# Router logits with the experts in the partitions, turned back by small products, and the key transposes behind the first gate product

## The chip, the cores and the metric

The kernel runs on one NeuronCore of one Trainium2 chip. A core has five engines that run their own instruction queues and wait for each other through semaphores: TensorE (PE in the profile, with its weight loads as PEld), VectorE (DVE), ScalarE (ACT), GpSimd (POOL) and SyncE (SP), which here only starts transfers. The metric is the time of one execution on the device, in microseconds; less is better. A "stationary" operand is the one that TensorE loads as weights, a "moving" operand is streamed past it.

## The reference

Sixteen sequences of 256 tokens with 256 channels go through an attention layer and then a mixture of experts, each with a residual sum. What matters for this change is the router, which for each token gives eight logits:

```python
logits_h = x @ wt.T                       # x: tokens x 256, wt: 8 x 256
logits_g = jnp.repeat(g @ wg.T, s, axis=0)
logits = (logits_h + logits_g / GE_TEMP) / (1.0 + 1.0 / GE_TEMP)
scores = jax.nn.softmax(logits, axis=-1)
topk_w, topk_idx = jax.lax.top_k(scores, K)      # K = 2, then normalised
```

The experts (eight, and two shared blocks) are all computed, as gate, up and down products with a leaky ReLU between, and weighted by the router's result. Everything is float32. For the products of the attention, of the router and of the gate and up matrices the kernel splits each operand into a leading part "hi" and a rest "lo" of a type that TensorE takes at full rate, and sums hi·hi + lo·hi + hi·lo.

## The kernel before

The 4096 tokens are worked in eight rounds of 512 tokens (four tiles of 128, `TILES`), two sequences a round. Attention of round r and the experts of round r - 1 are interleaved by hand: each engine has one function `attention(r, moe, following)`, which issues the attention's instructions of round r and, between them, those of the experts of round `moe` = r - 1. Round 0 is written out with no experts, rounds 1 to 6 are one hardware loop, round 7 is written out again, and the experts of round 7 follow alone (the tail). Nothing but this written order and the semaphores sets when an instruction runs.

At the head of each round, on TensorE: the normalised tokens `x1` of the round before are turned (`turn_x1`, L1405) into banks psG and psO; queries of tile 1 (`q_half`, L63 to L65 through the helper `products`) and half of tile 2; the router's `logits`; four transposes of the keys `kd` into psO (L1271), which first wait until VectorE has read the logits out of psG and psO; the first block's gate product (`gate(moe, 0)`) into psG; the second half of query tile 2; the first up product (`up(moe, 0)`); and so on up to the score loop, which takes most of a round (`score`, `turn`, `value`, with the rest of the experts between).

The logits before the change: for each of 4 tiles and 2 channel halves three products with the tokens stationary (128 x 128) and 256 columns of `Wall` moving, of which the first 8 are the router's; 24 products. They stand with tokens in the partitions, so that the softmax over experts runs along the free axis.

VectorE at the same place: keys normalised into `kd`, `MK`, then `router_logits` (L1077 twice adds `cond_logits`, L1081 takes the maximum, L1082 subtracts it: `lgc<-lg,lgx`, both inputs in SBUF), `sum_q` of query tile 1 (L1017), the key parts `KB` (L902, L906), `leak(0)` (L1132), `hidden(0)` (L1142), `sum_q` of tile 2, `router_best`, and further to the first `scores` (L1042), where the score loop begins for it.

ScalarE: `route` (x1T), squares and copies of query tile 0 and 1 (L619, L623), `softmax` (L696), key copy (L628), `take_gate(0)` (L707), query tile 2. GpSimd: powers `rk` and `rq` (L541), then `scale_q` of tile 0 (L385, 128 x 1024, both inputs in SBUF), and in the score loop the normalisation of the attention's rows. `scale_q` of tile 0 starts after the power of tile 0, which starts after VectorE's `sum_q` of tile 0.

SyncE's queue matters in the tail: `experts` loads gate and up weights when the up product that used their buffer is done, then writes the router's weights `WT` to memory and reads them back broadcast, row by row, as `Wb`.

## Time and profile before

| | us |
|---|---|
| median of 3 timed runs | 1135.3 |
| lowest, highest | 1133.45, 1136.15 |
| the profiled execution | 1139.32 |
| its span, first to last instruction | 1137.4 |
| PE busy in the span | 1028.3 (90%) |
| PEld, DVE | 843.4, 781.0 |
| ACT, POOL | 526.0, 443.3 |
| mean granted TensorE clock | 0.976 of full |

The profile is of one execution, which took 4.0 us more than the median of the timed ones. Busy shares are averages over stages; what bounds a stage is read from the timeline of that stage, where each row may carry the idle time in front of it and the engine that ended it.

### The profile page before, as it was taken

To read this page: it belongs to the slowest core of one execution; us is meant where nothing else is said; L and a number is where in the kernel's file an instruction comes from. 1 tells how busy PE (TensorE), PEld (TensorE's weight loads), DVE (VectorE), ACT (ScalarE), POOL (GpSimd) and SP (SyncE) were. 2 spreads that over 40 slices of the span, in tenths; PEclk is the share of its full clock that TensorE was granted. 3 is DMA by queue.
4 is the path that set the end of the run, shared out by engine and by line. 5 is a ranking of instruction groups with operands and counts; after the bars stand their busy time and mean duration, and the time that the engine had idled before them with its cause. 6 is when DMAs were issued, how large, how long until landed. Compare 5 with 4: busy or idle time off the path is not lost.

```text
span 1137.4 us, 22612 instructions
## 1 busy us (share of the span) xinstructions
PE 1028.3 (90%) x7340; PEld 843.4 (74%) x7340; DVE 781.0 (69%) x2538; ACT 526.0 (46%) x1563; POOL 443.3 (39%) x422
## 2 busy tenths in 40 slices
PE   2377899999999999899999999899998999999898
PEld 1265587777877788677877787777877778777777
DVE  6768858775687648775587747876597756866442
ACT  2048724663356614655255623565146642566111
POOL 3154414553435505453336424354145433355112
PEclk9688999999999999999999999999999999999999
DMA  5064411321123212321123111221113211232033
GB/s 203 19 177 158 150 38 56 104 85 57 40 80 98 66 40 74 103 66 38 58 91 96 59 55 58 92 68 65 59 56 103 84 38 33 81 103 65 20 104 119
DMA packets 40939, 89.89 MB, mean 79 GB/s; under 512 B 4128, under 2 KB 18976, under 8 KB 40304
## 3 DMA queue, kind: packets, MB, share of 16 engines
q1 hardware_dynamic: 40816, 88.29, 24.3%
q8 instruction: 73, 1.20, 0.5%
q14 instruction: 50, 0.41, 0.1%
HBM read 78.67 MB, written 11.70 MB: 79 GB/s over the span
## 4 chain that ended last, share of the span: by engine, by line
PE 66%; DVE 20%; issue 6%; ACT 5%; POOL 1%; DMA 1%; SPq 1%; DVEq 0%; ACTq 0%; POOLq 0%
PE psY L1460 11%; PE psO L1393 6%; PE psS L1363 5%; PE psG L63 4%; PE psG L65 4%; PE psG L64 4%; PE psT L1374 3%; PE psS L63 3%; PE psS L64 3%; DVE work L1042 3%; PE psS L65 3%; PE psS L1358 2%; PE psO L1396 2%; PE psT L63 2%; PE psT L65 2%
## 5 line engine op out<-in xcount | busy, mean ns | idle before, releaser
L552 POOL TENSOR_TENSOR work<-work,rden 128x514 f32<-128x514 f32 x128 | 134.3, 1049 | 329.1 <-DVE rden L1023 328.5
L1460 PE MATMUL psY<-Wd,H 128*128 128x256 f32 x640 | 166.7, 395 | 3.7 <-POOL H L566 3.7
L675 ACT ACTIVATE work<-work,low 128x257 f32<-128x257 f32 x256 | 128.3, 503 | 80.7 <-DVE low L1042 80.6
L63 PE MATMUL psG<-x1T_hi,Wgu 128*128 128x512 f32 x280 | 128.1, 458 | 11.7 <-ACT leaky L707 9.8
L1460 PEld LDWEIGHTS psY<-Wd,H 128*128 128x128 f32 x640 | 113.3, 189 | 32.3 <-issue 15.6
L1042 DVE CUSTOM_DVE_ANT_0 work<-psS,bias,null_s 128x256 f32<-128x256 f32 x256 | 113.0, 478 | 18.3 <-PE psS L1363 18.0
L1132 DVE SCALAR_TENSOR_TENSOR leaky<-leaky 128x512 f32<-128x512 f32 x80 | 55.6, 695 | 101.5 <-ACT leaky L707 100.5
L541 POOL TENSOR_TENSOR rq<-qss,neghalf 128x16 f32<-128x16 f32 x32 | 93.7, 2930 | 55.0 <-DVE qss L1017 55.0
L65 PE MATMUL psG<-x1T_lo,Wgu 128*128 128x512 f32 x280 | 110.3, 394 | 0.0
L64 PE MATMUL psG<-x1T_hi,Wgu 128*128 128x512 f32 x280 | 109.6, 391 | 0.0
L667 ACT ACTIVATE qT_hi<-psO 128x256 fp32r<-128x256 f32 x128 | 48.9, 382 | 108.8 <-PE psO L1396 107.7
L679 ACT ACTIVATE work<-work,low 128x129 f32<-128x129 f32 x256 | 99.2, 389 | 0.0
L566 POOL TENSOR_TENSOR H<-H,Wb 128x512 f32<-128x512 f32 x64 | 82.5, 1289 | 41.9 <-DMA Wb<-wscr 30.0
L1393 PE MATMUL psO<-PTs,kvs 128*64 128x256 f32 x512 | 84.0, 405 | 10.6 <-DVE qT_lo L1069 10.6
L687 ACT ACTIVATE PTs<-psT 128x512 f32<-128x512 f32 x128 | 75.3, 588 | 35.7 <-PE psT L1374 35.6
L558 POOL TENSOR_TENSOR rstd<-ve,neghalf 128x1 f32<-128x1 f32 x32 | 17.5, 546 | 186.9 <-DVE ve L987 186.9
L1363 PE MATMUL psS<-KB_hi,qT_hi 64*128 64x256 f32 (+1 forms) x512 | 84.5, 321 | 0.0
L1374 PE MATMUL psT<-ident,work 128*128 128x128 f32 x512 | 78.0, 275 | 5.3 <-ACT PTs L687 4.2
L554 POOL TENSOR_TENSOR work<-work,rden 128x258 f32<-128x258 f32 x128 | 79.4, 620 | 0.0
L1069 DVE TENSOR_TENSOR qT_lo<-psO,qT_hi 128x256 fp32r<-128x256 f32 x128 | 53.7, 420 | 37.2 <-ACT qT_hi L667 37.2
L1048 DVE CUSTOM_DVE_ANT_0 work<-psS,bias,null_s 128x128 f32<-128x128 f32 x256 | 78.9, 345 | 0.0
L1374 PEld LDWEIGHTS psT<-ident,work 128*128 128x128 f32 x512 | 62.2, 140 | 22.5 <-issue 7.9
(242 smaller groups left out, 2677.4 us busy)
## 6 DMA issues: line engine op xcount, KB each, us to landing
Wgu<-wexp SPq DMA_DIRECT2D x80, 512.0 KB, 3.5
Wb<-wscr SPq DMA_DIRECT2D x64, 256.0 KB, 3.7
wexp<-Wgu SPq DMA_DIRECT2D x10, 512.0 KB, 2.9
xin<-in_x SPq DMA_DIRECT2D x8, 512.0 KB, 4.1
xres<-in_x SPq DMA_DIRECT2D x8, 512.0 KB, 5.0
out<-work SPq DMA_DIRECT2D x8, 512.0 KB, 3.1
H<-in_wgu SPq DMA_DIRECT2D x10, 256.0 KB, 3.8
bscr<-bscr SPq DMA_DIRECT2D x1, 2048.0 KB, 13.0
```

The costliest lines, as they stand in the source:

```text
L63: te.matmul(dst, a_hi, b_hi, start=start, stop=False)
L64: te.matmul(dst, a_lo, b_hi, start=False, stop=False)
L65: return te.matmul(dst, a_hi, b_lo, start=False, stop=stop)
L541: pool.tensor_tensor(rq[:, t, :], qss[:, t, :], neghalf[:], ALU.pow).then_inc(rq_done.sem, 1)
L552: pool.tensor_tensor(T1[sl][:, hs, :], T1[sl][:, hs, :], rden[sl][:, 1, hs].unsqueeze(2) .to_broadcast([P, 2, N + 1]), ALU.mult)
L675: act.activation(T1[sl][:, h, :], T1[sl][:, h, :], ACT.Exp, scale=-1.0, bias=low[sl][:, 1, h:h + 1], accum_out=den[sl][:, 1, h:h + 1])
L679: last = act.activation(T0[sl][:, h, :], T0[sl][:, h, :], ACT.Exp, scale=-1.0, bias=low[sl][:, 0, h:h + 1], accum_out=den[sl][:, 0, h:h + 1])
L1042: ins = dve.tensor_tensor_reduce(T1[sl][:, h, 0:N], psS[:, i, 0:N], bias[:, h0 + h, :], 1.0, null_s[:, 2 * bb + 1, h0 + h:h0 + h + 1], ALU ...
L1363: mm = te.matmul(psS[:, i, first:first + keys_], qT[a][half, p, q1:q1 + P], KB[b][half, bb, 0:keys_], start=False, stop=(first == N and b ...
L1374: mm = te.transpose(psT[:, 0, (2 * i + j) * P:(2 * i + j + 1) * P], T1[sl][:, 2 * s + i, j * P:(j + 1) * P], ident[:])
L1393: te.matmul(psO[i * DH:(i + 1) * DH, 0:N], kvs[:, 2 * bb, DH:2 * DH], PT[n % 2][:, i, 0:N], start=True, stop=False)
L1460: mm = te.matmul(psY[:, t // 2, (t % 2) * D:(t % 2 + 1) * D], H[:, k % H_RING, t * P:(t + 1) * P], Wd[:, ORDER[k], :], start=(k == 0 and t ...
```

## The change

The router's weights get a tile of their own, `WtP`, with the 8 hi and the 8 lo columns side by side. They become stationary and the 512 tokens stream past: two products of 16 columns with `x1T` hi (one per channel half) and two of 8 columns with `x1T` lo, all into psO, 16 partitions x 512 tokens. ScalarE copies these to `LT` in SBUF. Four small float32 products with `LT` stationary and `I2` (two 8 x 8 identities on top of each other, so that it also adds the hi and the lo rows) moving give 128 tokens x 8 experts per tile, in psY. The first gate product stands between the logits and these small products; the key transposes come behind them. On ScalarE the new copy stands where the softmax stood, and the softmax moves behind `take_gate(0)`. In the tail VectorE issues `leak(0)` ahead of `router_best` and `hidden(0)` ahead of `router_weights`, and ScalarE's `softmax` and `weights` stand behind its first and second gate copy. One small VectorE instruction that makes `I2` is added to the preparation.

```diff
@@ -135,8 +135,10 @@
-        Wall = [sb(f"Wall_{part}", [P, KC, E + KVN + HEADS * DH], F32R) for part in PARTS]
-        KV0, Q0 = E, E + KVN
+        Wall = [sb(f"Wall_{part}", [P, KC, KVN + HEADS * DH], F32R) for part in PARTS]
+        KV0, Q0 = 0, KVN
+        WtP = sb("WtP", [P, KC, 2 * E], F32R)
+        I2 = sb("I2", [2 * E, E])[:]
...
+        LT = sb("LT", [2 * E, TOK])[:]
+        WT = LT[0:E, :]
...
@@ act: attention
                     if t >= 2 and moe is not None:
                         take_gate(moe, t - 2)
+                        if t == 2:
+                            softmax(moe)
...
                     if t == 1:
                         if moe is not None:
-                            softmax(moe)
+                            logits(moe)
...
+            def logits(m):
+                need(act, lt_ps, m, 1)
+                need(act, wscr_in, m - 1, 16)
+                act.activation(LT, psO[0:2 * E, :], ACT.Copy).then_inc(lt_done.sem, 1)
...
             route(ROUNDS - 1)
-            softmax(ROUNDS - 1)
-            weights(ROUNDS - 1)
+            logits(ROUNDS - 1)
             for k in range(BLOCKS):
                 take_gate(ROUNDS - 1, k, True)
+                if k == 0:
+                    softmax(ROUNDS - 1)
+                if k == 1:
+                    weights(ROUNDS - 1)
...
@@ dve: preparation, router_logits, tail
                 dve.wait_ge(pre_t.sem, 4)
+                pre(dve.tensor_tensor(I2, ident[0:2 * E, 0:E], ident[0:2 * E, E:2 * E], ALU.add))
...
-                for i, bank in enumerate((psG, psO)):
+                for i in range(BB):
                     ins = dve.tensor_tensor(
-                        lg[:, 2 * i:2 * i + 2, :], bank[:, :].rearrange("p (t c) -> p t c", t=2)[:, :, 0:E],
+                        lg[:, 2 * i:2 * i + 2, :], psY[:, 0, 2 * i * E:2 * (i + 1) * E].rearrange("p (t e) -> p t e", t=2),
...
             router_logits(m)
+            leak(m, 0)
             router_best(m)
+            hidden(m, 0, True)
             router_weights(m)
-            for k in range(BLOCKS):
+            for k in range(1, BLOCKS):
...
@@ te: attention
                 if moe is not None:
                     logits(moe)
+                    gate(moe, 0)
+                    turn_logits(moe)
                 need(te, kd_done, r, 1)
-                if moe is not None:
-
-                    te.wait_ge(vchain["router"].ev.sem, vchain["router"].ev.at(moe, 1))
...
                 mm.then_inc(kdT_ps.sem, 1)
-                if moe is not None:
-                    gate(moe, 0)
                 q_half(2, 1).then_inc(q_ps.sem, 1)
...
             def logits(m):
+
                 need(te, x1T_v, m, 3)
+                for c in range(KC):
+                    te.matmul(psO[0:2 * E, :], WtP[:, c, :], x1T[0][:, c, :], start=(c == 0), stop=False, skip_group_check=True)
+                for c in range(KC):
+                    mm = te.matmul(psO[0:E, :], WtP[:, c, 0:E], x1T[1][:, c, :], start=False, stop=(c == KC - 1),
+                                   skip_group_check=True)
+                mm.then_inc(lt_ps.sem, 1)
+
+            def turn_logits(m):
+
+                need(te, lt_done, m, 1)
+                need(te, ysum, m - 1, TILES)
                 for t in range(TILES):
-                    for c in range(KC):
-
-                        mm = products(te, (psG, psO)[t // 2][:, (t % 2) * 2 * P:(t % 2 + 1) * 2 * P],
-                                      [part[:, c, t * P:(t + 1) * P] for part in x1T],
-                                      [part[:, c, 0:2 * P] for part in Wall], c == 0, c == KC - 1)
+                    mm = te.matmul(psY[:, 0, t * E:(t + 1) * E], LT[:, t * P:(t + 1) * P], I2, start=(t == 0), stop=True,
+                                   skip_group_check=True)
                 mm.then_inc(lg_ps.sem, 1)
...
                 gate(m, k, True)
+                if k == 0:
+                    turn_logits(m)
                 up(m, k, True)
```

TensorE in the loop's round, before: the last tile's logits, then the key transposes, then the first gate product.

```order
L63 MATMUL psO<-Wall_hi,x1T_hi 128x256
L64 MATMUL psO<-Wall_hi,x1T_lo 128x256
L65 MATMUL psO<-Wall_lo,x1T_hi 128x256
L86 REGISTER_ALU
L1269 ISA
L1271 MATMUL psO<-ident,kd 128x128 x4
L86 ISA x2
L63 MATMUL psG<-x1T_hi,Wgu 128x512
```

The same place with the change (the first operand listed is not always the stationary one):

```order
L1427 MATMUL psO<-x1T_hi,WtP 16x512 x2
L1429 MATMUL psO<-x1T_lo,WtP 8x512 x2
L86 ISA x2
L63 MATMUL psG<-x1T_hi,Wgu 128x512
L64 MATMUL psG<-x1T_hi,Wgu 128x512
L65 MATMUL psG<-x1T_lo,Wgu 128x512
...
L1438 MATMUL psY<-I,LT 128x8 x4
L86 REGISTER_ALU
L1288 MATMUL psO<-ident,kd 128x128 x4
L63 MATMUL psT<-Wall_hi,xnT_hi 128x512
```

The gate product moved ahead of the key transposes, and what VectorE waits for (the end of L1438) now stands behind the gate product and behind a ScalarE copy.

ScalarE in the loop's round, before, from the copy of query tile 1 to the square of tile 2:

```order
L623 ACTIVATE work<-psS 128x1024
L696 ACTIVATE lex<-lgc 128x32
L86 REGISTER_ALU
L628 ACTIVATE KB_hi<-psO 64x512
L86 ISA
L707 ACTIVATE leaky<-psG 128x512
L86 REGISTER_ALU
L619 ACTIVATE work<-psT 128x1024
```

and with the change:

```order
L630 ACTIVATE work<-psS 128x1024
L86 ISA
L705 ACTIVATE LT<-psO 16x512
L86 REGISTER_ALU
L635 ACTIVATE KB_hi<-psO 64x512
L86 ISA
L719 ACTIVATE leaky<-psG 128x512
L709 ACTIVATE lex<-lgc 128x32
L86 REGISTER_ALU
L626 ACTIVATE work<-psT 128x1024
```

The copy to LT stands behind both large passes over query tile 1; the softmax moved behind the gate copy.

VectorE in the tail, before:

```order
L1082 TENSOR_TENSOR lgc<-lg,lgx 128x32
L1088 TENSOR_REDUCE lsum<-lex 128x4
...
L1099 MAX_INDEX topi<-top,score 128x8 x4
L1104 CAST topf<-topi 128x8
...
L1115 TENSOR_TENSOR oh<-wsel,trec 128x32
L1132 SCALAR_TENSOR_TENSOR leaky<-leaky 128x512
L1142 TENSOR_TENSOR H<-psS,leaky 128x512
```

and with the change:

```order
L1098 TENSOR_TENSOR lgc<-lg,lgx 128x32
L1148 SCALAR_TENSOR_TENSOR leaky<-leaky 128x512
L1104 TENSOR_REDUCE lsum<-lex 128x4
...
L1115 MAX_INDEX topi<-top,score 128x8 x4
L1158 TENSOR_TENSOR H<-psS,leaky 128x512
L1120 CAST topf<-topi 128x8
...
L1131 TENSOR_TENSOR oh<-wsel,trec 128x32
```

The first leaky ReLU and the first hidden product moved into the router's chain, ahead of the weights that TensorE's `turn_weights` waits for.

## Rows read from the trace of the kernel before

**Rows 1.** The page's chain that ended last: shares of the span by engine.
```profile
PE 66%; DVE 20%; issue 6%; ACT 5%; POOL 1%; DMA 1%; SPq 1%; DVEq 0%; ACTq 0%; POOLq 0%
```

**Rows 2.** Timeline, round 3: start us, us, engine, line, operation [idle before <-releaser]
```profile
430.78 0.28 PE L63 MATMUL psG<-Wall_hi,x1T_hi 128*128 128x256 f32 x1
...
433.96 0.17 DVE L1077 TENSOR_TENSOR lg<-psG,cond_logits 128x16 f32<-128x16 f32 x1 [0.68 <-PE psO L65]
...
434.35 0.66 PE L1271 MATMUL psO<-ident,kd 128*128 128x128 f32 x4 [0.54 <-DVE lg L1077]
434.55 0.19 DVE L1082 TENSOR_TENSOR lgc<-lg,lgx 128x32 f32<-128x32 f32 x1
...
434.87 1.91 POOL L385 TENSOR_TENSOR work<-work,rq 128x1024 f32<-128x1024 f32 x1
...
436.00 0.39 PE L65 MATMUL psG<-x1T_lo,Wgu 128*128 128x512 f32 x1
...
436.23 0.39 PE L63 MATMUL psT<-Wall_hi,xnT_hi 128*128 128x512 f32 x1
...
439.26 0.69 DVE L1142 TENSOR_TENSOR H<-psG,leaky 128x512 f32<-128x512 f32 x1 [0.50 <-PE psG L65]
```

**Rows 3.** Round 3, ScalarE's two passes over query tile 1, same columns.
```profile
431.78 1.03 ACT L619 ACTIVATE work<-psS 128x1024 f32<-128x1024 f32 x1 [2.99 <-DVE qss L1017]
...
432.71 1.02 ACT L623 ACTIVATE work<-psS 128x1024 f32<-128x1024 f32 x1
```

**Rows 4.** Groups by line: xcount | busy us, mean ns | idle before.
```profile
L701 ACT ACTIVATE WT<-psO 8x512 f32<-8x512 f32 x8 | 4.6, 573 | 4.9 <-PE psO L1421 4.9
```

**Rows 5.** Timeline of the preparation: float32 products with 16 moving columns.
```profile
48.44 1.89 PE L1186 MATMUL psT<-bias 128*128 128x16 f32 x8 [0.86 <-DVE bias L845]
```

**Rows 6.** Timeline, round 4: VectorE's logits beside GpSimd's scale_q, and hidden(0).
```profile
565.17 1.84 DVE L1082 TENSOR_TENSOR lgc<-lg,lgx 128x32 f32<-128x32 f32 x1
566.93 1.21 DVE L1017 TENSOR_REDUCE qss<-work 128x16 f32<-128x1024 f32 x1
...
571.06 0.69 DVE L1142 TENSOR_TENSOR H<-psG,leaky 128x512 f32<-128x512 f32 x1
...
565.05 1.91 POOL L385 TENSOR_TENSOR work<-work,rq 128x1024 f32<-128x1024 f32 x1
```

**Rows 7.** Timeline, round 2: the same two instructions.
```profile
304.37 0.19 DVE L1082 TENSOR_TENSOR lgc<-lg,lgx 128x32 f32<-128x32 f32 x1
...
304.52 1.91 POOL L385 TENSOR_TENSOR work<-work,rq 128x1024 f32<-128x1024 f32 x1
```

**Rows 8.** Timeline: VectorE's first scores in rounds 2, 3, 4; last x1 tile of round 3.
```profile
325.00 0.48 DVE L1042 CUSTOM_DVE_ANT_0 work<-psS,bias,null_s 128x256 f32<-128x256 f32 x1
...
455.18 0.48 DVE L1042 CUSTOM_DVE_ANT_0 work<-psS,bias,null_s 128x256 f32<-128x256 f32 x1
...
586.94 0.48 DVE L1042 CUSTOM_DVE_ANT_0 work<-psS,bias,null_s 128x256 f32<-128x256 f32 x1
...
554.80 0.49 DVE L994 SCALAR_TENSOR_TENSOR x<-x,rstd,xres 128x256 f32<-128x256 f32 x1 [0.34 <-POOL rstd L558]
```

**Rows 9.** Timeline, round 1: hidden(0).
```profile
178.51 0.69 DVE L1142 TENSOR_TENSOR H<-psG,leaky 128x512 f32<-128x512 f32 x1 [0.30 <-PE psG L65]
```

**Rows 10.** Timeline, the tail: logits, router chain, turn_weights, the third gate product.
```profile
1081.63 0.58 PE L63 MATMUL psG<-Wall_hi,x1T_hi 128*128 128x256 f32 x1 [1.98 <-DVE x1T_lo L1126]
...
1087.51 0.19 DVE L1088 TENSOR_REDUCE lsum<-lex 128x4 f32<-128x32 f32 x1 [0.30 <-ACT lex L696]
...
1090.93 0.19 DVE L1115 TENSOR_TENSOR oh<-wsel,trec 128x32 f32<-128x32 f32 x1
...
1091.55 0.53 PEld L1421 LDWEIGHTS psO<-ident,oh 128*8 128x8 f32 x4
...
1093.59 0.19 PEld L63 LDWEIGHTS psT<-x1T_hi,Wgu 128*128 128x128 f32 x1 [1.51 <-issue]
```

**Rows 11.** Stretch: us, each engine's busy us, granted TensorE clock, DMA share, GB/s.
```profile
1081.60:1085.40 3.80, 3.77 (x17) 3.77 (x18) 0.00 (x0) 0.00 (x0) 0.00 (x0) 0.50 0.00 0
```

## What the change will do to the time

> **What bounds the kernel now.** I read the chain of waits first: 66% of it is TensorE, 20% VectorE [rows 1]. That is a mean over stages, so the next view is the timeline of one loop round (round 3) from the logits on. TensorE issues the 24 logit products from 430.78; the last result frees VectorE at 433.96, after 0.68 us of idle time there, and the key transposes then wait 0.54 us for VectorE [rows 2]. So far TensorE leads. Then comes what decides. VectorE's next idle time is 0.50 us in front of `hidden(0)` at 439.26 [rows 2]. From there to its first `scores` at 455.18 [rows 8] it is idle only for hand-offs of 0.15 to 0.20 us in its own chains. So the stretch from 434 to 455 is VectorE's: TensorE could gain there 0.50 us of waiting that VectorE has, and no more.
>
> A second reading is in round 4. `lgc<-lg,lgx`, which takes 0.19 us in round 3, took 1.84 us, from 565.17 to 567.01. GpSimd's `scale_q` ran from 565.05 to 566.96 [rows 6]. In rounds 2 and 3 the same instruction began at 304.37 and 434.55, that is 0.15 and 0.32 us before `scale_q` at 304.52 and 434.87, and was not held [rows 2, 7]. Rounds 5 and 6 read like round 4, and in the written-out rounds 1 and 7 it came late in `scale_q` and was held briefly, to the same end. The sum over two inputs `lgc` therefore cannot run while `scale_q` does; the reduction behind it can (in round 3 it did), and so can the additions in front, which read one input from PSUM.
>
> The Trainium skill ("SBUF — State Buffer", section "Who interferes with whom") says why: a VectorE instruction with two SBUF inputs and a GpSimd instruction that reads SBUF want the same read port, and whichever starts first blocks the other for its whole length. By that rule, the trace agrees, with ends 0.05 us apart in round 4. It speaks against this change, since what counts is the order of the two starts. Nothing below needs this paragraph.
>
> What the hold costs: from the end of `scale_q` to the first scores are 586.94 - 566.96 = 19.98 us in the held round 4, with no idle time before `hidden(0)` [rows 6, 8]; rounds 5 and 6 give the same. In round 2 they are 325.00 - 306.43 = 18.57, in round 3 455.18 - 436.78 = 18.40 [rows 2, 7, 8]. So a hold costs 1.41 or 1.58 us. It is carried to the round's end: from the first scores to the last `x1` tile are 554.80 - 455.18 = 99.62 us in round 3 [rows 8], and 99.6 in each loop round, held or not.
>
> **The change, part by part.**
> - Logits, TensorE: 24 products of 256 columns at (433.96 - 0.42 - 430.78) / 23 = 0.12 us, 2.9 us in all [rows 2], where 0.42 is the last product's 0.28 and a hand-off of 0.14. They become 4 products of 512 columns at 436.23 - 436.00 = 0.23 us [rows 2], 0.9 us. TensorE saves 2.0 us a round, and the 0.54 us wait.
> - The added path: the logits are ready at about 430.78 + 0.9 + 0.3 = 432.0, but ScalarE is in its passes over query tile 1 until 432.71 + 1.02 = 433.73 [rows 3]. The copy to LT then takes 0.57 us, by the copy of 8 x 512 [rows 4], to 434.25. TensorE has finished the first gate product (431.7 + 6 x 0.23 = 433.1) and waits about 1.2 us. Queued behind that wait are the key transposes and `q_half`; VectorE waits in `router_logits`, with `sum_q` of tile 1 behind it.
> - The four small products: 4 float32 products with few columns are 8 instructions, which took 1.89 us at half clock in the preparation [rows 5], so some 1.0 us at full. The other bound is the transposes of keys, 4 in 0.66 us [rows 2]. No row has 8 columns from 16 partitions; I take 1.0, the nearest kind. The logits reach VectorE at 435.0 to 435.4, against 433.96: 1.0 to 1.4 us later.
> - What VectorE meets there: `lgc` starts 0.59 us behind (434.55 - 433.96 [rows 2]), at 435.6 to 436.0. GpSimd's `scale_q` runs from 434.87 to 436.78 and is not touched by the change. So `lgc` is held until 436.8, whichever bound is right. ScalarE's passes and `scale_q` both start from the same `sum_q` of tile 0, so this comes out the same in every loop round: **all five loop rounds with late starts (2 to 6) are held**, instead of three of five.
> - Sum for the rounds, on the profiled execution: rounds 2 and 3 lose 1.41 + 1.58 = 3.0 us; rounds 4 to 6 lose nothing, as VectorE leaves `lgc` at the same moment. In round 1 `scale_q` ends at about the moment at which the new `lgc` ends, and VectorE's 0.30 us of waiting before `hidden(0)` [rows 9] goes, since the up product is earlier; in round 7 it is 0.1. That gives back 0.4. TensorE's own 2.0 us a round are lost in waits for ScalarE and, at the second gate product, for VectorE's `hidden(0)`.
> - The moved softmax costs nothing: `router_best` reads it more than 4 us later. The new wait of the first down product on the router's first link is over 10 us old by then; likewise `ysum` before the small products.
> - Tail: the logits start at 1081.63 [rows 10], and the 24 products took to 1086.4. The granted clock was 0.50 of full (1.2 GHz) until 1085.4 [rows 11], after TensorE had waited. The four long ones take 4 x 0.43 = 1.8 us with the first start, to 1083.5. The gate product, four sixths at half clock, ends at 1085.85; the small products 1.0 later, VectorE's logits at 1086.95 against 1086.51. Its chain to the weights was 1091.12 - 1087.51 = 3.6 us [rows 10]; now `leak(0)` and `hidden(0)` lie inside it, 0.69 us each [rows 2], so the weights are done at about 1092.5. TensorE waits for them from 1090.8 and starts the third gate product at 1092.95, where it started at 1093.59 after a wait for ScalarE's gate copies [rows 10]. Gain 0.65; the transfer of the weights follows the third up product and moves by 0.9, so it does not take it back. I take 0.7, bounds 0.3 (if the small products are slower than thought) and 1.3 (the whole wait of 1.51 less a hand-off).
> - Preparation: one more small VectorE instruction in a chain in which each waits for the last. One with two small SBUF inputs takes 0.19 [rows 2]. I add 0.2.
>
> Sum on the profiled execution: 3.0 - 0.4 - 0.7 + 0.2 = +2.1 us, 1139.3 to 1141.4.
>
> **From there to the median.** The timed runs are 4.0 us shorter at the median and lie 2.7 us apart. The hold of the old kernel is decided by 0.1 to 0.3 us between two starts, so it will differ from run to run: five rounds, about 1.45 us each. With three held rounds in the median run the change costs 2.1, with two 3.5, with none 6.4, with all five it gives 0.8. Three missing holds would explain the 4.0 us alone, which speaks for few. I take two: 1135.3 + 3.5 = **1138.8**. A measurement can tell about 0.2%, 2.3 us: slower begins at 1137.6.
>
> **Rivals.**
> - The old kernel is held in three to five rounds when timed as well. Then +2.1 to -0.8, 1134.5 to 1137.4, within 0.2%. The profile (three of five) is for it, the shorter timed runs against.
> - TensorE is the bound after all. Place: the second half of query tile 2, at 436.23 before. It would start when the small products and key transposes are done, at about 435.5, so 0.7 earlier; seven rounds give 4.9, with tail and preparation 5.4: 1129.9. It decides only if VectorE is not later than before at `hidden(0)`. Against it: VectorE's time from `lgc` on has 0.5 us of air at most.
> - The idle gaps. TensorE now stops for 1.2 us in front of the small products and again at the second gate product. In the tail it came back at half clock after a wait of 1.98 us, the second of its kind in a row, and stayed there for 3.8 us; after the wait of 1.51 us it ran at full [rows 10, 11]. If the gaps bring that to seven rounds, 3.8 us at half speed is 1.9 us of work each, of which VectorE's lead hides some: up to 8 more, 1147.
> - The change does not do what it says about the hold (`lgc` slips in before `scale_q`): it would have to start before 434.87, hence need ScalarE 0.8 us sooner than its own rows allow. Then rounds 2 and 3 lose nothing, and 4 to 6 win 1.4 each: 1130.5.
>
> **Chances.** Forecast with at most two held rounds before: 0.53. Held three to five: 0.28. TensorE the bound: 0.09. Gaps: 0.06. No hold: 0.04. Faster by over 0.2%: 0.13; within 0.2%: 0.29; slower: 0.58. The range takes in none to all five held rounds and half of an error in the tail: 1133.9 to 1142.0.
>
> **What would show it.** Right: `lgc` of rounds 2 to 6 takes 1 us or more and ends within 0.1 us of `scale_q`; 19.98 us from there to the first scores; a loop round of 131.7 us throughout; VectorE's wait before `hidden(0)` gone; TensorE idle about 1.2 us before the small products. Wrong: `lgc` at 0.19 us; small products well over 1.0 us, when VectorE would leave after `scale_q`'s end and each tenth costs seven; a clock below full in the head of the rounds; or a tail that did not shorten.

## The result, and the profile after

| | median us | lowest to highest | runs |
|---|---|---|---|
| before | 1135.72 | 1133.03 to 1136.65 | 6 |
| after | 1139.09 | 1138.22 to 1139.21 | 6 |

The ratio is 1.0034, with a 95% interval of 1.0021 to 1.0047: slower, by 3.4 us. Forecast were 1138.8 us and "slower". A second comparison, on the chip of the last four experiments, gave 1.0038 (1.0023 to 1.0052).

The profiled execution of after took 1139.09 us with a span of 1137.3, so it is a typical one. That of before took 1139.32 and is not: it is 3.6 us above the median, so the two traces seem to show no loss at all. They have to be read by stage.

The chain of waits, to compare with [rows 1]; shares of the span:

```profile
PE 59%; DVE 24%; issue 8%; ACT 5%; POOL 1%; DVEq 1%; SPq 1%; DMA 0%; ACTq 0%; POOLq 0%
```

TensorE's share fell from 66% to 59% and VectorE's rose from 20% to 24%. The work moved onto the engine that bounds the stretch.

The timeline of round 3, to compare with [rows 2]: start in us, duration in us, engine, line, operation, [idle before <-releaser]. L1427 and L1429 are the long logit products (two each, so the first row stands for a pair), L705 the copy to LT, L1438 the eight instructions of the four small products, L390 `scale_q`, L1033 `sum_q`, L1158 `hidden(0)`, L1058 the first scores:

```profile
432.45 0.62 PE L1427 MATMUL psO<-x1T_hi,WtP 128*16 128x512 f32 x2
...
434.41 0.57 ACT L705 ACTIVATE LT<-psO 16x512 f32<-16x512 f32 x1
...
435.03 1.05 PE L1438 MATMUL psY<-I,LT 16*128 16x8 f32 x8
...
436.24 0.33 DVE L1093 TENSOR_TENSOR lg<-psY,cond_logits 128x16 f32<-128x16 f32 x2 [2.15 <-PE psY L1438]
...
436.82 0.80 DVE L1098 TENSOR_TENSOR lgc<-lg,lgx 128x32 f32<-128x32 f32 x1
...
435.67 1.90 POOL L390 TENSOR_TENSOR work<-work,rq 128x1024 f32<-128x1024 f32 x1
...
437.54 1.20 DVE L1033 TENSOR_REDUCE qss<-work 128x16 f32<-128x1024 f32 x1
...
441.67 0.69 DVE L1158 TENSOR_TENSOR H<-psG,leaky 128x512 f32<-128x512 f32 x1
...
442.42 0.50 PE L63 MATMUL psG<-x1T_hi,Wgu 128*128 128x512 f32 x1 [1.53 <-DVE H L1158]
...
457.54 0.48 DVE L1058 CUSTOM_DVE_ANT_0 work<-psS,bias,null_s 128x256 f32<-128x256 f32 x1
```

`scale_q` runs from 435.67 to 437.57. `lgc` starts inside it, at 436.82, and ends 0.05 us behind it, at 437.62, though alone it needs 0.19 us. From the end of `scale_q` to the first scores are 457.54 - 437.57 = 19.97 us. `hidden(0)` has no wait in front of it, where 0.50 us stood before; TensorE has one of 1.53 us at the second gate product, for VectorE.

The same instruction over the whole program (xcount: shortest/median/longest in ns), before and then after:

```profile
L1082 DVE TENSOR_TENSOR lgc<-lg,lgx x8: 191/486/1889, 173.8 to 1087.0; 128x32 f32<-128x32 f32 x8
```

```profile
L1098 DVE TENSOR_TENSOR lgc<-lg,lgx x8: 192/794/799, 174.0 to 1088.4; 128x32 f32<-128x32 f32 x8
```

All five loop rounds 2 to 6 are held. A short name for what follows: the **head** of a round is the time from the start of `scale_q` to the first scores. It is worked out from such pairs of rows; in rounds 2 to 6 it is

| | round 2 | 3 | 4 | 5 | 6 |
|---|---|---|---|---|---|
| before (h = held) | 20.48 | 20.31 | 21.89 h | 21.89 h | 21.88 h |
| after, all held | 21.89 | 21.87 | 21.88 | 21.87 | 21.88 |

From the first scores of one round to `scale_q` of the next the two kernels hardly differ: 109.9 us from round 2 on before (565.05 - 455.18 [rows 6, 8]), 109.8 to 110.1 after. So the head is where the rounds differ.

The tail, to compare with [rows 10]: first long logit product, `lg`, `turn_weights`, third gate product:

```profile
1083.18 1.04 PE L1427 MATMUL psO<-x1T_hi,WtP 128*16 128x512 f32 x2 [1.98 <-DVE x1T_lo L1142]
...
1093.41 0.60 PE L1445 MATMUL psO<-ident,oh 128*8 128x128 f32 x4 [1.21 <-DVE oh L1131]
...
1093.77 0.48 PE L63 MATMUL psT<-x1T_hi,Wgu 128*128 128x512 f32 x1
```

```profile
1087.93 0.26 DVE L1093 TENSOR_TENSOR lg<-psY,cond_logits 128x16 f32<-128x16 f32 x2 [4.80 <-PE psY L1438]
...
1088.44 0.19 DVE L1098 TENSOR_TENSOR lgc<-lg,lgx 128x32 f32<-128x32 f32 x1
```

From the first logit product to the third gate product are 1093.77 - 1083.18 = 10.6 us, where 12.0 stood before.

And one difference that is not the change's. In round 7 the granted clock fell in the profiled execution of before during the output projection (stretch, the engines' busy us, granted clock, DMA share, GB/s; before first, then after):

```profile
1060.00:1064.00 4.00, 3.07 (x18) 2.99 (x17) 1.74 (x5) 0.38 (x1) 0.00 (x0) 0.71 0.18 59
...
1064.00:1068.00 4.00, 4.00 (x30) 3.94 (x30) 1.30 (x5) 0.00 (x0) 0.55 (x1) 0.87 0.22 72
```

```profile
1060.00:1064.00 4.00, 2.04 (x20) 1.35 (x20) 2.11 (x6) 0.96 (x3) 0.00 (x0) 1.00 0.02 4
...
1064.00:1068.00 4.00, 4.00 (x35) 3.95 (x34) 1.50 (x5) 0.00 (x0) 0.00 (x0) 1.00 0.37 131
```

So the traces add up: at the head of round 7 after is 2.6 us behind (first scores 982.50 against 979.88). It gets about 1.1 us back from that dip, up to the tail's logits (1083.18 against 1081.63), 1.4 in the tail up to the third gate product and another 0.3 behind it (43.5 us to the end of the span, where 43.8 stood before), and ends level. The profiled execution of before was long for its three held rounds and its dip; the median of before has less of them. What that "less" is, the experiments had to say.

### The profile page after: what moved, and what is told of

Its sections match the earlier page's. It is cut to its first block, busy times and chain, and to the rows that moved or that the text cites. A ratio compares the mean times of both kernels' runs of the same rounds, so it can differ in the third digit from the quotient of the medians.

```text
span 1137.3 us, 22424 instructions
## 1 busy us (share of the span) xinstructions
PE 1020.5 (90%) x7244; PEld 827.4 (73%) x7244; DVE 778.7 (68%) x2539; ACT 529.3 (47%) x1571; POOL 442.7 (39%) x422
## 4 chain that ended last, share of the span: by engine, by line
PE 59%; DVE 24%; issue 8%; ACT 5%; POOL 1%; DVEq 1%; SPq 1%; DMA 0%; ACTq 0%; POOLq 0%
PE psY L1481 11%; PE psO L1408 6%; PE psS L1378 5%; PE psG L63 4%; PE psG L65 3%; PE psT L1389 3%; PE psG L64 3%; DVE work L1058 3%; PE psO L1411 2%; DVE work L390 2%; PE psS L1373 2%; PE psS L63 2%; PE psS L64 2%; PE psS L65 2%; DVE qss L1033 2%
## 5 line engine op out<-in xcount | busy, mean ns | idle before, releaser
L1058 DVE CUSTOM_DVE_ANT_0 work<-psS,bias,null_s 128x256 f32<-128x256 f32 x256 | 113.0, 477 | 18.6 <-PE psS L1378 18.1
L63 PEld LDWEIGHTS psG<-x1T_hi,Wgu 128*128 128x128 f32 x280 | 52.6, 188 | 40.1 <-DVE H L1158 15.3
```

Of the source, the lines that this page charges most:

```text
L63: te.matmul(dst, a_hi, b_hi, start=start, stop=False)
L1058: ins = dve.tensor_tensor_reduce(T1[sl][:, h, 0:N], psS[:, i, 0:N], bias[:, h0 + h, :], 1.0, null_s[:, 2 * bb + 1, h0 + h:h0 + h + 1], ALU ...
```

## The experiments

Theory A: the time is decided by whether `lgc`, with two inputs in SBUF, meets `scale_q`. Rival B: a later logit costs time by itself. Rival C: TensorE's waits or its clock cost the time. Rival D: TensorE is the bound. The kernels of one group ran on one chip beside the kernel before. Where two experiments of a group are compared, the interval is the 95% one of the difference of medians, from random redraws of the two sets of times.

**Group 1.** The kernel before again, for a profile.

> The kernel before, unchanged, for another profiled execution. Theory A (the extra time of the change is the lgc subtraction held behind the scaling of query tile 0 in all five rounds 2 to 6, while the kernel before is held in some of them): this execution differs from the first profiled one in the number of held rounds (lgc of 1.4 to 1.9 us instead of 0.19), by about 1.5 us of time for each, and in the clock of the last round's projection. An execution near 1135.7 shows about two held rounds, one near 1133 none. Rival B (the delay of the logits is paid directly, holds play no part): the time is not related to the number of held rounds.

This execution took 1135.44 us. `lgc` was held in rounds 2 and 6, and not in 3, 4 and 5. Round 2 held, round 3 not:

```profile
303.44 1.90 POOL L385 TENSOR_TENSOR work<-work,rq 128x1024 f32<-128x1024 f32 x1
...
303.62 1.77 DVE L1082 TENSOR_TENSOR lgc<-lg,lgx 128x32 f32<-128x32 f32 x1
...
435.14 0.19 DVE L1082 TENSOR_TENSOR lgc<-lg,lgx 128x32 f32<-128x32 f32 x1
...
435.23 1.91 POOL L385 TENSOR_TENSOR work<-work,rq 128x1024 f32<-128x1024 f32 x1
```

Two held rounds near 1135.7, as expected, and other rounds than in the first profile: the outcome of a race between two starts 0.1 to 0.4 us apart. But this execution is 3.9 us shorter than the first one, and the hold is only part of that: the heads of rounds 2 to 6 are 1.45 us shorter in sum. Of the rest 0.9 us lie in front of round 1's `scale_q` (171.39 against 172.25) and 1.7 us between the first scores of round 7 and the tail's logits (100.08 against 101.75), where the clock dipped in the first profile. One execution more is thin evidence for a count, so the next two runs take the hold away.

**`lg` in PSUM, in either kernel.** The subtraction then has one SBUF input (`lgx`). In the changed kernel:

```diff
-        lg = sb("lg", [P, TILES, E])
+        lg = psY[:, 1, 0:TILES * E].rearrange("p (t e) -> p t e", t=TILES)
...
-                    te.wait_ge(vchain["router"].ev.sem, vchain["router"].ev.at(m, 1))
+                    te.wait_ge(lg_done.sem, lg_done.at(m, 1))
```

The second pair is the wait of the first down product, which writes that bank. In the kernel before that wait is added to the one on `ysum`.

> The changed kernel with lg written to PSUM, so that the lgc subtraction has only one input in SBUF; the first down product waits for lgc as well. Theory A: lgc takes 0.19 to 0.25 us in every round and starts beside the scaling of query tile 0 (GpSimd, 1.9 us) without waiting for it; the first scores come 0.5 to 0.6 us earlier in each of rounds 2 to 6, so 2.5 to 3.0 us less than the changed kernel: about 1136.2. Rival B (a later logit costs time by itself, whatever inputs lgc has): lgc stays at 0.8 us or its end gains nothing, the time stays at 1139.1. Rival C (the time is lost on TensorE, in its waits and its clock): the time stays at 1139.1, since TensorE's order is unchanged.

> The kernel before with the same edit: lg in PSUM, nothing else. Theory A: no round is held, every loop round is as long as an unheld one of the first profile (scaling of query tile 0 to first scores 20.48 us instead of 21.89), and all executions lie at the lowest of the kernel before, about 1133.0 to 1133.6, with a narrow spread; against the median of the kernel before 2 to 3 us less. Rival B: the same median and the same spread as the kernel before, 1133.0 to 1136.7.

| group 1 | median us | lowest to highest | ratio to before (95%) |
|---|---|---|---|
| before (29 runs) | 1136.42 | 1132.32 to 1141.48 | |
| after, lg in PSUM (12) | 1135.79 | 1134.52 to 1137.86 | 1.0000 (0.9984 to 1.0015) |
| before, lg in PSUM (12) | 1133.89 | 1131.91 to 1135.28 | 0.9983 (0.9966 to 1.0000) |
| after, LT copied twice (12) | 1139.12 | 1137.22 to 1140.76 | 1.0027 (1.0011 to 1.0042) |

Round 3 of the changed kernel with `lg` in PSUM:

```profile
435.48 1.90 POOL L390 TENSOR_TENSOR work<-work,rq 128x1024 f32<-128x1024 f32 x1
...
436.64 0.19 DVE L1098 TENSOR_TENSOR lgc<-psY,lgx 128x32 f32<-128x32 f32 x1
...
436.75 1.21 DVE L1033 TENSOR_REDUCE qss<-work 128x16 f32<-128x1024 f32 x1
...
456.77 0.48 DVE L1058 CUSTOM_DVE_ANT_0 work<-psS,bias,null_s 128x256 f32<-128x256 f32 x1
```

`lgc` starts 1.16 us into `scale_q` and still takes 0.19 us. The head is 21.29 us in each of the five rounds, 0.59 less than 21.88. Nothing moved but where one operand lies, and the hold is gone: that is shown, and it is against B and C, by which the time would have stayed. (The Trainium skill, "SBUF — State Buffer", section "Who interferes with whom", states that a VectorE instruction with at most one SBUF input does not contend with GpSimd outside its two-port modes; the trace agrees, with 0.19 us in all eight places.) Five times 0.59 is 2.95 us; the median is 3.3 below that of the changed kernel in the first comparison (another chip).

The kernel before with the same edit has `lgc` at 0.19 us in all eight places and heads of 20.31 to 20.54 us. Its median is just above the 1133.0 to 1133.6 us that I named. Its spread is 3.4 us in 12 runs, where the kernel before has 9.2 in 29 on that chip: a large part of the old kernel's unrest was the hold, though not all unrest is (the copy ahead with `lg` in PSUM, below, cannot be held and has 6.4). What the hold cost the old kernel at the median is 2.5 us here and 1.0 in the last group. A held round there costs less than the 1.45 us of the prediction, which compared it with rounds in which `lgc` started ahead of `scale_q`. With `lg` in PSUM and `lgc` 0.12 us behind the start of `scale_q` the head is 20.75 us (round 5 of the second such profile), 1.1 less than a held one. So the two costs stand for 0.9 to 2.2 held rounds. Each interval of the ratio just touches 1, so the size is rough.

The two edits side by side give the price of the change without any hold: 1135.79 - 1133.89 = 1.9 us (1.0 to 3.4). That is the part of B that is true. The head is 21.29 against 20.3 to 20.5 us, because `lgc` itself comes 1.3 to 1.5 us later against `scale_q`, and VectorE had only 0.50 us of air. Five times 0.85, less what rounds 1 and 7 and the tail give back in these two profiles (0.2 and 1.5), is 2.5 us.

**The logits later still.**

```diff
+        LTx = sb("LTx", [2 * E, TOK])
...
+                act.activation(LTx[:], psO[0:2 * E, :], ACT.Copy)
                 act.activation(LT, psO[0:2 * E, :], ACT.Copy).then_inc(lt_done.sem, 1)
```

> The changed kernel, in which ScalarE copies the turned logits out of PSUM twice, first to a scratch tile: the logits come another 0.57 us later in every round. Theory A: in rounds 2 to 6 lgc still ends with the scaling of query tile 0, so nothing is lost there; the first and last rounds and the tail pay up to 0.57 us each: 0.5 to 1.7 us more, 1139.6 to 1140.8. Rival B (the delay is paid one for one): 8 x 0.57 = 4.6 us more, about 1143.6.

1139.12 us, and a ratio of 1.0027 where the change alone has 1.0034: nothing was lost, not even the 0.5 us that I allowed for the first and last rounds and the tail (the heads of rounds 1 and 7 are 22.09 and 21.64 us, with the change alone 22.08 and 21.62). The rows of round 3:

```profile
434.48 0.57 ACT L706 ACTIVATE LTx<-psO 16x512 f32<-16x512 f32 x1
...
434.96 0.57 ACT L707 ACTIVATE LT<-psO 16x512 f32<-16x512 f32 x1
...
437.37 0.32 DVE L1100 TENSOR_TENSOR lgc<-lg,lgx 128x32 f32<-128x32 f32 x1
```

`lgc` starts 0.55 us later than in the changed kernel (437.37 against 436.82) and ends at the same distance from `scale_q`, which ran from 435.74 to 437.64; it is only held for less (0.32 instead of 0.80). The heads are 21.88 to 21.95 us. Inside the hold a delay is free. B asked for 4.6 us, and falls. Against the changed kernel without the hold this one is 3.3 us slower (1.9 to 4.1), on the same chip.

**Group 2. The logits earlier.** ScalarE copies to LT ahead of its passes over query tile 1, and the small products go ahead of the first gate product:

```diff
                     need(act, q_ps, r, t + 1)
+                    if t == 1 and moe is not None:
+                        logits(moe)
...
                     if t == 1:
-                        if moe is not None:
-                            logits(moe)
...
-                    gate(moe, 0)
                     turn_logits(moe)
+                    gate(moe, 0)
```

> The changed kernel with ScalarE's copy of the turned logits put ahead of its two passes over query tile 1, and the small products ahead of the first gate: the logits reach VectorE about 1.3 us earlier in each of rounds 2 to 6, while lg stays in SBUF. Theory A: lgc starts some 0.2 us before the scaling of query tile 0 and takes 0.19 us; the scaling to the first scores falls from 21.88 to 20.0 to 20.6 us in these rounds, 6.4 to 9 us in all: 1130.1 to 1132.7. If lgc lands just behind the start of the scaling in some rounds, it is held for 1.9 us there and each such round gives the gain back. Rival B (any delay is paid one for one): 5 x 1.3 = 6.5 us less too, but lgc's own duration would not matter. Rival D (TensorE or ScalarE is the bound): the time does not fall, since TensorE now waits for the copy with nothing to do and ScalarE's passes over tile 1 come 0.6 to 1.1 us later.

> Both edits: the copy and the small products ahead, and lg in PSUM. Theory A: no hold is possible, so every round 2 to 6 takes 20.0 to 20.6 us from the scaling of query tile 0 to the first scores whatever the jitter, 3.5 to 6.5 us less than with lg in PSUM alone: 1129.5 to 1132.5, narrow, and below both kernels. Rival (the early copy delays something else on ScalarE, which then comes last): no faster than with lg in PSUM alone, 1135.8.

"Keys first" and "old tail" in the table are the two experiments behind these two.

| group 2 | median us | lowest to highest | ratio to before (95%) |
|---|---|---|---|
| before (23 runs) | 1134.79 | 1131.42 to 1138.99 | |
| copy ahead (12) | 1139.22 | 1134.83 to 1141.64 | 1.0034 (1.0018 to 1.0050) |
| copy ahead, lg in PSUM (12) | 1133.63 | 1130.02 to 1136.46 | 0.9987 (0.9972 to 1.0001) |
| keys first (6) | 1142.80 | 1141.37 to 1145.79 | 1.0075 (1.0055 to 1.0095) |
| old tail (6) | 1140.00 | 1139.03 to 1143.04 | 1.0051 (1.0031 to 1.0070) |

With `lg` in SBUF the earlier copy won nothing. The second of my two cases came: `lgc` landed just behind the start of `scale_q`. Rounds 3 and 5:

```profile
434.49 1.91 POOL L390 TENSOR_TENSOR work<-work,rq 128x1024 f32<-128x1024 f32 x1
...
434.66 1.79 DVE L1098 TENSOR_TENSOR lgc<-lg,lgx 128x32 f32<-128x32 f32 x1
...
698.00 0.19 DVE L1098 TENSOR_TENSOR lgc<-lg,lgx 128x32 f32<-128x32 f32 x1
...
698.01 1.94 POOL L390 TENSOR_TENSOR work<-work,rq 128x1024 f32<-128x1024 f32 x1
```

0.17 us too late is held for 1.60 us, and the head is 21.89; 0.01 us ahead is not held, and the head is 20.17. Rounds 3, 4 and 6 were held, 2 and 5 not. The same order with `lg` in PSUM is 5.6 us faster (3.7 to 7.3): one operand's place is worth more than the whole change. This settles A against B once more, since the logits come at the same time in both.

It was less than I expected, though: I named 1129.5 to 1132.5 us and measured 1133.63. The heads were 19.97, 21.92, 20.42, 19.91 and 20.53 us. In rounds 4 and 6 `lgc` started 0.27 and 0.37 us behind `scale_q`, which makes the head longer by as much without any hold. Round 3 shows what came in the way, key transposes on TensorE (L1288) and VectorE's copy of them (L918), and the granted clock from 435.5 to 437.9:

```profile
432.47 1.05 PE L1438 MATMUL psY<-I,LT 16*128 16x8 f32 x8 [0.83 <-ACT LT L705]
...
434.95 1.04 PE L1288 MATMUL psO<-ident,kd 128*128 128x128 f32 x4
...
436.02 0.69 DVE L918 CAST KB_hi<-psO 64x512 fp32r<-64x512 f32 x1 [0.43 <-PE psO L1288]
```

```profile
435.50:437.90 2.40, 2.40 (x8) 1.94 (x7) 1.91 (x4) 1.19 (x3) 2.40 (x2) 0.50 0.01 3
```

TensorE waited for the copy with nothing in front, and 2.5 us after it went on it was at 1.2 GHz; the transposes took 1.04 us, where the same four took 0.60 in round 5, and VectorE waited 0.43 us for them and 1.14 at `hidden(0)`. The wait of 0.83 us stands in every loop round of this kernel, and the clock fell in this one alone. So rival C is real here, now and then.

In the changed kernel the first gate product covers most of that wait, and the clock was 1.00 from 433.30 to 437.80. It is not immune: in the 30 loop rounds of the six profiles with its TensorE order the clock fell in four heads (two of the kernel with two copies, one in each of the two old-tail kernels), behind waits of 0.93 to 1.36 us in front of the small products. This is round 2 of the second old-tail profile:

```profile
304.62 1.05 PE L1434 MATMUL psY<-I,LT 16*128 16x8 f32 x8 [0.97 <-ACT LT L705]
```

```profile
306.00:309.20 3.20, 3.20 (x10) 2.63 (x9) 3.07 (x7) 1.28 (x4) 1.94 (x2) 0.50 0.03 8
```

It cost next to nothing: the heads of these four rounds are 21.89 to 21.95 us, against 21.87 to 21.90 of the held ones at full clock, and TensorE's wait at the second gate product (1.1 to 1.6 us in the other rounds) is gone in them. TensorE had that much slack, and used it.

**The gate product back behind the key transposes,** which undoes the second half of the change's title:

```diff
-                    gate(moe, 0)
                     turn_logits(moe)
...
                 mm.then_inc(kdT_ps.sem, 1)
+                if moe is not None:
+                    gate(moe, 0)
                 q_half(2, 1).then_inc(q_ps.sem, 1)
```

> The changed kernel with the first gate product back behind the key transposes, as in the kernel before: TensorE waits idle for ScalarE's copy of the turned logits (1.5 to 2 us a round) and the gate's 1.15 us come later. Theory A (the stretch is bound by VectorE): ScalarE's copy sets when the logits are turned, so lgc starts when it did and nothing is lost in rounds 2 to 6 unless the later first gate delays the first leak: within 1 us of 1139.1. Rival D (TensorE is the bound): 1.15 us a round, 7 us more, 1146.

1142.80 us: a miss for both. Against the changed kernel, by the ratios to before, it is 4 to 5 us slower, where I allowed 1 and the rival wanted 7. The rows of round 3, and the clock behind the small products:

```profile
435.89 1.05 PE L1439 MATMUL psY<-I,LT 16*128 16x8 f32 x8 [1.65 <-ACT LT L705]
...
443.39 0.69 DVE L1158 TENSOR_TENSOR H<-psG,leaky 128x512 f32<-128x512 f32 x1 [0.89 <-PE psG L65]
```

```profile
437.80:441.40 3.60, 3.60 (x10) 2.81 (x9) 3.51 (x5) 1.08 (x3) 2.35 (x2) 0.53 0.01 2
```

TensorE waits 1.65 us, is at half clock in nearly all of this stretch, and the first up product comes too late: VectorE waits 0.89 us at `hidden(0)`. The heads of rounds 2 to 5 are 22.79 to 22.84 us, 0.9 to 1.0 more than held ones. In round 6 TensorE waited as long (1.63 us), but the clock stayed at full, and the head is 21.90, no longer than a held one. So the order alone costs nothing, as theory A had it; the order and the half clock together used up TensorE's slack in four rounds of five, and that is what both expectations had left out. The move of the transposes behind the gate is what keeps the change from being slower still.

**The tail.** The changed kernel with the old order of the tail, in group 2 and again in group 3 beside the changed kernel itself:

```diff
             logits(ROUNDS - 1)
+            softmax(ROUNDS - 1)
+            weights(ROUNDS - 1)
             for k in range(BLOCKS):
                 take_gate(ROUNDS - 1, k, True)
-                if k == 0:
-                    softmax(ROUNDS - 1)
-                if k == 1:
-                    weights(ROUNDS - 1)
...
-            leak(m, 0)
             router_best(m)
-            hidden(m, 0, True)
             router_weights(m)
-            for k in range(1, BLOCKS):
+            for k in range(BLOCKS):
```

> The changed kernel with the old order in the tail: ScalarE does softmax and weights before its first gate copy, VectorE all of the router before the first leak. The rounds are untouched, so only what lies behind the tail's logits can differ. My prediction took 0.7 us for the tail (0.3 to 1.3); the two traces show 1.4 us less from the start of the tail's logits to the third gate product. If the new tail order is what gives it, this run is 0.7 to 1.4 us slower than the changed kernel, 1139.8 to 1140.5, and the stretch is back at about 12 us. Rival (the 1.4 us come from the shorter logits and from the clock, not from the order): within 0.3 us of 1139.1, the stretch stays at 10.6 us.

> The changed kernel, unchanged, on the same chip as the three runs that follow, and for a second profiled execution. Theory A: again all of rounds 2 to 6 are held (lgc 0.79 to 0.80 us, 21.88 us from the scaling of query tile 0 to the first scores). The time against the kernel before: a ratio of 1.003 to 1.004.

> The changed kernel with the old order in the tail, now beside the changed kernel on the same chip. If the tail's order gives 0.7 us (my term): about 0.7 us slower than the changed kernel. If it gives the 1.4 us that the two traces show: 1.4 us slower. If the 1.4 us came from the clock: within 0.3 us, with the third gate product again behind a wait of 1.25 us.

| group 3 | median us | lowest to highest | ratio to before (95%) |
|---|---|---|---|
| before (35 runs) | 1133.81 | 1131.12 to 1139.12 | |
| after (12) | 1138.97 | 1136.65 to 1140.55 | 1.0038 (1.0023 to 1.0052) |
| after, old tail (12) | 1139.97 | 1137.85 to 1141.64 | 1.0049 (1.0035 to 1.0064) |
| before, lg in PSUM, new tail (12) | 1134.36 | 1132.11 to 1136.28 | 0.9987 (0.9971 to 1.0004) |
| before, lg in PSUM (12) | 1132.78 | 1131.72 to 1135.15 | 0.9988 (0.9974 to 1.0003) |

In group 2 the old order stood at 1140.00 us, inside what I had named, but without the changed kernel beside it, and its profile can't be used: it had half clock until 1092.7, and the stretch took 13.7 us, not 12. In group 3 the old order is 1.0 us slower (0.1 to 2.5). The timing can't tell 0.7 from 1.4; the traces can. The changed kernel again, and then with the old order:

```profile
1084.67 1.03 PE L1427 MATMUL psO<-x1T_hi,WtP 128*16 128x512 f32 x2 [1.98 <-DVE x1T_lo L1142]
...
1089.97 0.19 DVE L1098 TENSOR_TENSOR lgc<-lg,lgx 128x32 f32<-128x32 f32 x1
...
1095.30 0.47 PE L63 MATMUL psT<-x1T_hi,Wgu 128*128 128x512 f32 x1
```

```profile
1083.59 1.03 PE L1423 MATMUL psO<-x1T_hi,WtP 128*16 128x512 f32 x2 [1.98 <-DVE x1T_lo L1140]
...
1089.39 0.19 DVE L1096 TENSOR_TENSOR lgc<-lg,lgx 128x32 f32<-128x32 f32 x1
...
1095.40 0.47 PE L63 MATMUL psT<-x1T_hi,Wgu 128*128 128x512 f32 x1 [1.25 <-ACT leaky L719]
```

From `lgc` to the third gate product: 1095.30 - 1089.97 = 5.33 us with the new order, 1095.40 - 1089.39 = 6.01 with the old. The order gives 0.68 us up to here, and more behind it: from the third gate product to the end of the span are 43.5 us in all seven profiles with the new logits and the new order, 43.95 in this one and 43.7 in that of group 2. For this pair that makes 1.2 us in all, near the 1.0 us of the timing. In front of `lgc` the code is the same in both, and the distances from the first logit product are 5.30 and 5.80: there the clock differs from run to run, and in the run of group 2 with the old order it was 6.80. All five loop rounds of the changed kernel were held again (0.80 us each; heads of 21.87 to 21.89).

**The old logits with the new tail order,** from the kernel before with `lg` in PSUM; the edit is the reverse of the one above.

> The kernel before with lg in PSUM and the new tail order (first gate copy ahead of softmax on ScalarE, first leak and first hidden tile among the router's steps on VectorE); the logits are computed as before. No lgc is held. The tail's third gate product waits 1.25 us for the first gate copy in the kernel before; with the new order that wait goes and a wait of up to 1.2 us for the router's weights is left in its place. Expected 0.3 to 0.9 us less than with lg in PSUM alone, and 2.5 to 3.5 us less than the kernel before: the fastest of the family, 1132 to 1133.6. Rival (the router's end sets the third gate product whichever comes first): the same time as with lg in PSUM alone.

> The kernel before with lg in PSUM alone, on the same chip as the run with the new tail order, and for a second profiled execution. Theory A: again lgc takes 0.19 us in every round, rounds 2 to 6 take 20.3 to 20.6 us from the scaling of query tile 0 to the first scores, and the ratio to the kernel before is 0.997 to 0.999.

The second is as expected (`lgc` 0.19 us everywhere, a ratio of 0.9988), but for heads of 20.44 to 20.75 us, a little over the 20.6 I named. The first is a miss: 1.6 us slower, if anything (-0.3 to 2.9). VectorE's rows in its tail:

```profile
1081.98 0.18 DVE L1079 TENSOR_TENSOR psY<-psG,cond_logits 128x16 f32<-128x16 f32 x1 [5.58 <-PE psO L65]
...
1084.34 0.69 DVE L1134 SCALAR_TENSOR_TENSOR leaky<-leaky 128x512 f32<-128x512 f32 x1 [1.65 <-ACT leaky L707]
```

With the old logits the first gate product is behind all logits, so the first leak, now ahead of the router's steps, waits 1.65 us for it, and the whole router stands behind that wait. From the first logit product to the third gate product it takes 13.1 us, where 11.8 stand with the old order. Not all of this is the order's: in front of `lgc`, where the code is the same, 0.84 us of it lie (6.05 against 5.21 us, with half clock until 1082.6 here, 6.1 us from the first product, and for 3.4 us there). From `lgc` to the third gate product it is 7.07 us against 6.58, so the order costs 0.5 us there, where with the new logits it gained 0.68; behind that product this profile is 0.6 us shorter again. The new order pays up to the third gate product only because the new logits let the first gate product run before the logits are turned; whether it costs anything by the end with the old logits is not shown.

## Why the prediction was right, point by point

- **VectorE bounds the stretch.** Right, shown by the head: it follows the end of `lgc`, or of the hold, at 19.9 to 20.0 us wherever VectorE has no wait (19.97 after, 19.94 with `lg` in PSUM), however much TensorE saved. The 0.50 us of air [rows 2] was all that the change could use. Four heads of the changed order at half clock that were no longer than the others say the same.
- **The hold, and that all five loop rounds get it.** Right, and its cause is shown by the place of one operand. "With ends 0.05 us apart" holds in the changed kernel too (437.57 and 437.62).
- **Where the logits arrive.** Right within 0.1 us at its late end: with the round 0.8 us later than before, I had 435.8 to 436.2 for VectorE's logits, and they came at 436.24. The small products took 1.05 us, 1.0 was taken. One step on the way was wrong and cost nothing: the long products began 0.9 us later than I had them (432.45), since TensorE stood still for 0.84 us, "issue" (a wait for nothing that the profile shows), in front of the loop round's first instruction. ScalarE's passes set the time of the copy all the same. Two of my signs were wrong with it. TensorE hardly waited in front of the small products: 0.10 us in round 3 and 0.7 at most in the loop rounds of this profile, not 1.2. And `lgc` took 0.80 us, not "1 us or more".
- **The sum for the rounds.** +3.0 - 0.4 on the profiled execution; at the first scores of round 7 after is 2.62 us behind. The +3.0 is right: the heads of rounds 2 to 6 are 2.9 us longer. The -0.4 came out in part by luck: the heads of rounds 1 and 7 give back 0.14 (22.19 to 22.08, 21.65 to 21.62), since `lgc` of round 1 also ended 0.2 us later against `scale_q`. The other 0.26 us lie in front of round 1's `scale_q` (171.99 against 172.25), where two profiles of one kernel differ by more (171.99 and 172.98 after, 172.25 and 171.39 before).
- **The tail.** Mis-sized: 0.7 was predicted, with 1.3 as the bound; the traces show 1.4 up to the third gate product and 1.7 to the end, outside it. The new order's part is 0.68 us to the third gate product and 1.2 to the end; I had put nothing behind the third gate product. Of my error up to there, most lies in front of VectorE's logits: I put VectorE's logits 0.44 us later than before (1086.95 against 1086.51) and they came 0.1 us earlier, 4.75 us after the first product instead of 4.88. I had kept the half clock for 3.8 us, as before [rows 11]. It lasted 2.8 us here (it read 0.50 from 1083.10 to 1085.90, and 1.00 soon after). In the other profiles with the changed kernel's tail it lasted 2.7 to 4.5 us, so this part can differ from run to run.
- **From the profile to the median.** The step with the least ground, and the one on which the number hung: I took two held rounds in the timed runs of before, because three missing holds would explain the 4.0 us. That reason was wrong: of the 3.9 us between the two profiles of before, the holds are 1.45. The count was near all the same, which is in part luck: the second profile of before, at 1135.44 us, had two, and the kernels with `lg` in PSUM say 0.9 to 2.2. By those the rounds would bring the sum to 3.2 to 5.1 us instead of 3.5, with the tail's 1.0 less and the 0.3 more of rounds 1 and 7 to 2.5 to 4.4: 3.4 measured in the first comparison, 5.2 by the medians (4.3 by the ratio) in the last. If fewer than two rounds were held, that error and the tail's had opposite signs; the number was nearer than its terms.
- **The rivals.** Not TensorE: it saved 2 us a round and waits 1.53 us at the second gate product. Not the gaps, in this kernel: neither of its two profiles has half clock in a head, and where its order had it (four rounds of other kernels) the head was not longer. They cost time only where TensorE's wait was left uncovered: in single rounds of the two kernels with the copy ahead, and in four rounds of keys first. Held in three to five rounds before: true of the profiled execution, not of the median. The price of "no hold", 1130.5, counted three rounds that win, as in the profile; with the two of my own forecast it is about 1.4 us higher.
- **What stays open.** Why the race before `lgc` comes out one way or the other in a given round is known by half. The "issue" gap at the loop round's first TensorE instruction varies from nothing to 0.5 us before and from 0.3 to 1.0 in the changed kernels, and it goes with the outcome. In the 25 loop rounds of the five profiles of the kernel before, with `lg` in SBUF or in PSUM, `lgc` starts 8.8 to 9.1 us after that instruction. With a gap of 0.31 us or less it starts ahead of `scale_q` (16 of 16 rounds), with 0.33 or more behind it (8 of 9). No run sets the gap, so that it is the cause is not shown, and what makes it is open. The row in question, round 3 of after:

```profile
427.37 0.65 PE L1420 MATMUL psG<-ident,x 128*128 128x128 f32 x4 [0.84 <-issue]
```

No version clearly beats the kernel before. `lg` in PSUM alone was at 0.9983 and 0.9988, with narrower spread; the copy ahead with `lg` in PSUM, and `lg` in PSUM with the new tail order, both at 0.9987.

## What to carry to other kernels

Before an instruction is moved, look at what runs on the other engines at its new place: a 0.19 us instruction with two SBUF inputs that starts just behind a long GpSimd instruction is as long as that one, and one operand in PSUM removes this. When an instruction's longest duration is several times its shortest at the same shape, its timing is a race, and the profiled execution is one draw of it: take the prediction's base from the timed runs, and ask how many draws they hold. Products taken from TensorE give nothing while VectorE's next wait for TensorE is shorter than what they took.

## What the hardware showed that I had not expected

- A hold of `lgc` by `scale_q` costs by where it starts: 0.17 us behind cost 1.60 us more of `lgc`, 1.16 us behind cost 0.61, 1.63 us behind 0.13, 0.01 us ahead nothing. `lgc` ends 0.04 or 0.05 us behind `scale_q` in every held case.
- In the last of these `scale_q` took 1.94 us instead of 1.90 or 1.91, in the one round where `lgc` started 0.01 us ahead of it. That the other engine gave way there is a guess from one round.
- Float32 products with 8 columns from 16 partitions cost 1.05 us for four, as eight instructions, 0.13 us each, and 1.87 us at half clock. Few columns do not make them cheap.
- TensorE's waits in front of the small products were followed by half clock in some rounds and not in others, 1.3 to 2.5 us after it went on: with 0.83 us (the two kernels with the copy ahead) in one loop round of five each, with 1.6 to 2.2 us (keys first) in four of five. A wait of 1.5 us at the second gate product of the changed kernel, in front of products with 512 columns, was not followed by it in any loop round of its two profiles: the granted clock was 1.00 from 442.4 to 450.0. What decides it was not tested.
- A stretch at half clock is not lost time by itself. In the changed kernel's order TensorE has 1.1 to 1.6 us of slack at the second gate product, and the four heads with such a stretch were at most 0.1 us longer.
